# A convolution-attention hybrid block: weighing two score tiles in a row in all eight attentions

## What is computed

```python
# first attention: projections to 32 channels, softmax over 1024 positions, residual
q, k, v = wq @ xf, wk @ xf, wv @ xf                   # (4, 32, 1024)
att = softmax(einsum('bmi,bmj->bij', k, q), axis=2)
x = x + wo @ einsum('bij,bmj->bmi', att, v)
t = x.reshape(4, 64, 1024).transpose(0, 2, 1)         # tokens, 64 channels
# second attention: of the normalised tokens with themselves
u = layernorm(t)
t = t + softmax(einsum('bqd,bkd->bqk', u, u), -1) @ u
# experts: top 2 of 8, gates from a softmax over router logits
w = layernorm(t)
top_p, top_i = top_k(softmax(w @ router_w + router_b), 2)
t = t + sum over the two of (top_p / sum(top_p)) * (w @ expert_w[e] + expert_b[e])
out = t.transpose(0, 2, 1).reshape(4, 64, 32, 32)
```

## Time and profile before

| | us |
|---|---|
| median of 3 runs | 241.38 |
| lowest and highest run | 240.24, 241.77 |
| the profiled execution, as a run | 242.07 |
| its span in the trace | 240.4 |
| TensorE matmuls busy | 215.7 |
| VectorE busy | 152.1 |
| ScalarE busy | 110.1 |
| GpSimd busy | 72.2 |

### The profile page before, as it was taken

One profiled execution on the slowest core, in us unless ns is written; L12 is line 12 of the kernel. 1 busy time (PEld: TensorE's weight loads), 2 busy tenths in 40 slices (PEclk: granted clock), 3 DMA queues, 4 the chain that ended last, 5 costly groups with the idle time before them and its releaser, 6 DMA issues.

```text
span 240.4 us, 2786 instructions
## 1 busy us (share of the span) xinstructions
PE 215.7 (90%) x987; PEld 100.9 (42%) x987; DVE 152.1 (63%) x364; ACT 110.1 (46%) x170; POOL 72.2 (30%) x88
## 2 busy tenths in 40 slices
PE   6999899899999998999899989999899996775494
PEld 1645344635343454243245433433433433353383
DVE  2689766568169686328965994484745365999070
ACT  2533545667854736564435266564546652020101
POOL 8030000160303000300333584003876300774940
PEclk9999999999999999999999999999999999988778
DMA  4770000000000000000000001000000200000021
GB/s 98 134 176 0 3 0 0 0 4 1 0 0 0 3 0 0 0 3 0 1 0 0 3 1 44 0 3 0 0 0 0 48 0 0 0 0 0 0 46 44
DMA packets 3341, 3.67 MB, mean 15 GB/s; under 512 B 2176, under 2 KB 2432, under 8 KB 3328
## 3 DMA queue, kind: packets, MB, share of 16 engines
q1 hardware_dynamic: 3328, 3.50, 6.8%
HBM read 2.45 MB, written 1.05 MB: 15 GB/s over the span
## 4 chain that ended last, share of the span: by engine, by line
PE 66%; DVE 19%; ACT 6%; issue 3%; POOL 3%; DMA 2%; SPq 0%; DVEq 0%; POOLq 0%
PE acc L498 24%; PE ring L491 7%; PE ring L473 6%; PE ring L550 5%; DVE rowmax L1059 5%; PE ring L551 4%; PE ring L592 2%; DVE prod L1200 2%; ACT prob L868 2%; PE ring L593 2%; DMA xin<-in_x 2%; PE ring L537 2%; PE ring L451 2%; PE ring L462 2%; PE ring L463 1%
## 5 line engine op out<-in xcount | busy, mean ns | idle before, releaser
L868 ACT ACTIVATE prob<-ring,shift 128x1024 f32<-128x1024 f32 x32 | 35.6, 1113 | 41.8 <-PE ring L551 41.8
L1059 DVE TENSOR_REDUCE rowmax<-ring 128x1 f32<-128x1024 f32 x32 | 38.2, 1219 | 10.1 <-PE ring L473 10.0
L373 POOL TENSOR_TENSOR sm<-sm,minus_half 128x8 f32<-128x8 f32 x8 | 15.8, 1974 | 86.7 <-DVE sm L1102 86.7
L865 ACT ACTIVATE prob<-ring 128x1024 f32<-128x1024 f32 x32 | 32.4, 1023 | 17.6 <-PE ring L491 17.5
L498 PE MATMUL acc<-prob,val 128*64 128x512 f32 x128 | 34.3, 616 | 2.4 <-ACT prob L865 2.4
L498 PE MATMUL acc<-prob,u 128*64 128x512 f32 x128 | 34.5, 618 | 0.3 <-ACT prob L868 0.3
L1200 DVE TENSOR_TENSOR prod<-ring,gate 128x1024 f32<-128x1024 f32 x16 | 19.3, 1218 | 14.5 <-PE ring L593 14.5
L550 PE MATMUL ring<-zst 128*128 128x512 f16 x64 | 24.6, 385 | 1.2 <-DVE rowmax L1059 1.2
L551 PE MATMUL ring<-zsw,zst 128*128 128x512 f16 x64 | 24.3, 379 | 0.0
L491 PE MATMUL ring<-kst,qst 98*128 98x512 f32 x64 | 21.7, 428 | 1.7 <-DVE kst L1072 1.2
L473 PE MATMUL ring<-qst,kst 96*128 96x512 f32 x64 | 22.6, 439 | 0.1
(11 more groups left out here) (152 smaller groups left out, 319.7 us busy)
## 6 DMA issues: line engine op xcount, KB each, us to landing
xin<-in_x SPq DMA_DIRECT2D x8, 256.0 KB, 4.1
out<-ob SPq DMA_DIRECT2D x6, 128.0 KB, 2.4
e_in<-in_L_ffn_expert_w SPq DMA_DIRECT2D x2, 128.0 KB
out<-ob SPq DMA_DIRECT2D x4, 64.0 KB, 2.0
eb_in<-in_L_ffn_expert_b SPq DMA_DIRECT2D x8, 2.0 KB
wo<-in_L_conv_wo SPq DMA_DIRECT2D x2, 8.0 KB, 2.4
r_in<-in_L_ffn_router_w SPq DMA_DIRECT2D x2, 2.0 KB
w<-in_L_conv_wq SPq DMA_DIRECT2D x1, 16.0 KB, 3.5
```

The source lines that it names most:

```text
L373: pool.tensor_tensor(sm[:, 3, :], sm[:, 2, :], minus_half[:, :], ALU.pow).then_inc(s_rs, 1)
L865: act.activation(prob1[:, j % DEEP, :], flat(filled(act, f"st{j}", b)), ACT.Exp).then_inc(s_p1, 1)
L868: act.activation(prob2[:, j % DEEP, :], flat(filled(act, f"s{j}", b)), ACT.Exp, bias=shift[:, :], accum_out=rsum2[b % 2][:, j:j + 1]).then ...
L1059: dve.tensor_reduce(rowmax[:, tile:tile + 1], flat(filled(dve, f"mx{tile}", b)), AX.X, ALU.max).then_inc(s_mx, 1)
```

## The change

Two weighings are put in a row everywhere, and the next two score tiles are placed ahead of each pair. `weigh_pair1` and `weigh_pair2` call `weigh1` and `weigh2` twice. The new order is written out for all stages; per pair (j, j + 1) it is: score tile j + 1, score tile j + 2, weighings j and j + 1. What was threaded in between stays in the same place of the ring's order, with one exception in FIRST, where a score tile and a maximum tile change places. The function `sixteen`, which nothing called, is removed. The lists of ScalarE, VectorE, GpSimd and SyncE are the same. The core of the diff:

```diff
-FIRST = [("st0", 0), ("st1", 0), ("mx0", 1), ("st2", 0), ("mx1", 1), ("mx2", 1), ("st3", 0), ("mx3", 1), ("st4", 0),
+FIRST = [("st0", 0), ("st1", 0), ("mx0", 1), ("st2", 0), ("mx1", 1), ("st3", 0), ("mx2", 1), ("mx3", 1), ("st4", 0),
...
+            def weigh_pair1(b, j):
+
+                weigh1(b, j)
+                weigh1(b, j + 1)
+
+            def weigh_pair2(b, j):
+                weigh2(b, j)
+                weigh2(b, j + 1)
...
             max_scores(1, 0)
-            weigh1(0, 0)
             scores1(0, 2)
+            weigh_pair1(0, 0)
             max_scores(1, 1)
-            weigh1(0, 1)
-            for j in range(3, T - 1):
-                max_scores(1, j - 1)
-                scores1(0, j)
-                weigh1(0, j - 1)
+            scores1(0, 3)
+            max_scores(1, 2)
+            max_scores(1, 3)
+            scores1(0, 4)
+            weigh_pair1(0, 2)
+            max_scores(1, 4)
+            scores1(0, 5)
+            max_scores(1, 5)
+            scores1(0, 6)
+            weigh_pair1(0, 4)
             max_scores(1, 6)
             scores1(0, 7)
             max_scores(1, 7)
-            weigh1(0, 6)
-            weigh1(0, 7)
+            weigh_pair1(0, 6)
...
             scores1(1, 0)
-            for j in range(1, 3):
-                scores1(1, j)
-                weigh1(1, j - 1)
+            scores1(1, 1)
+            scores1(1, 2)
+            weigh_pair1(1, 0)
             project_qk("q", 2)
             scores1(1, 3)
-            weigh1(1, 2)
             project_qk("k", 2)
             scores1(1, 4)
-            weigh1(1, 3)
+            weigh_pair1(1, 2)
             project_v(2)
             scores1(1, 5)
-            weigh1(1, 4)
             u_transposed(0)
...
+            max_scores(2, 0)
+            scores2(0, 2)
+            weigh_pair2(0, 0)
+            max_scores(2, 1)
+            scores2(0, 3)
+            max_scores(2, 2)
+            scores2(0, 4)
+            weigh_pair2(0, 2)
             max_scores(2, 3)
             scores2(0, 5)
             project_qk("q", 3)
             u_transposed(1)
-            weigh2(0, 4)
             max_scores(2, 4)
             scores2(0, 6)
+            weigh_pair2(0, 4)
             project_qk("k", 3)
-            weigh2(0, 5)
             max_scores(2, 5)
             scores2(0, 7)
             max_scores(2, 6)
-            weigh2(0, 6)
             max_scores(2, 7)
             project_v(3)
-            weigh2(0, 7)
+            weigh_pair2(0, 6)
...
                 scores1(b, 0)
-                for j in range(1, T):
-                    scores1(b, j)
-                    weigh1(b, j - 1)
-                    if b == 3 and j == 3:
-                        y_transposed(0)
-                    if j == 5:
-                        w_transposed(b - 2)
+                scores1(b, 1)
+                scores1(b, 2)
+                weigh_pair1(b, 0)
+                scores1(b, 3)
+                if b == 3:
+                    y_transposed(0)
+                scores1(b, 4)
+                weigh_pair1(b, 2)
+                scores1(b, 5)
+                w_transposed(b - 2)
+                scores1(b, 6)
+                weigh_pair1(b, 4)
+                scores1(b, 7)
                 route(b - 2)
...
             att2_transposed(2)
-            for j in range(2, T):
-                weigh2(3, j - 2)
-                scores2(3, j)
...
-            weigh2(3, 6)
-            weigh2(3, 7)
+            scores2(3, 2)
+            weigh_pair2(3, 0)
+            scores2(3, 3)
+            y_transposed(1)
+            scores2(3, 4)
+            weigh_pair2(3, 2)
+            scores2(3, 5)
+            w_transposed(2)
+            scores2(3, 6)
+            weigh_pair2(3, 4)
+            route(2)
+            scores2(3, 7)
+            weigh_pair2(3, 6)
```

## The result

The changed kernel takes 237.27 us (median of 4 runs, 236.11 to 238.88), the kernel before 240.81 (4 runs, 240.19 to 241.77): ratio 0.985, 95% interval 0.981 to 0.989. A second timing, of six runs beside eleven, gave 237.13 and 241.55: 0.981, interval 0.978 to 0.985; the ratio leaves out one slow run on either side (241.03 and 244.46, at a granted clock of 0.95). It is faster by 3.5 to 4.4 us. 235.6 was forecast, the range 232.5 to 240.5.

A forecast was written before the change was run, and what follows sets the result against it. TensorE, busy for 90% of the span, was taken as what matters. Merges save some 9.5 us there; after waits the stages sum to 5.8 off, so 241.4 - 5.8 = 235.6 us, range 232.5 to 240.5.

The forecast's parts named there:

- The price of a merge: TensorE: each of 30 merges of weighings saves 0.35 us, or 0.25 before an fp16 tile.
- Image 0's second attention loses: Waits on row maxima and q's and k's buffers lose 3.2 us there; image 2's score tile 0 comes 2.46 late.
- The four waits: In image 0's second attention, TensorE idles 1.45, 1.3, 1.2 and 0.65 us before tiles whose buffers are not yet free.
- The stages without maxima: First attentions of images 2 and 3, without row maxima: the sum counts gains of 2.5 and 1.9 us.
- The rival that ScalarE delays the second weighing of each pair: In stages without maxima, exponentials keep twelve pairs' second weighings waiting 0.3 us each: 239.2 us; chance 0.16.
- Image 1's second attention and the last two: Second attentions: image 1's gains 0.6 us through three merges; those of images 2 and 3 gain 3.2 together.
- nothing is added: On TensorE and elsewhere: every matmul, exponential and row maximum stays, and as many bytes move.
- Image 0's first attention: Two full cycles lose 0.19 us each through a 0.54 wait on a maximum; shorter end groups return it: 0.
- The sum of 5.8: Gain in us over all stages, 0.0 + 0.8 - 3.2 + 2.5 + 0.6 + 1.9 + 3.2, off the profiled span of 240.4.
- the chance of 0.04 that I gave the clock: Rival: new pauses slow TensorE's clock, losing half the 6.1 us the tail loses: 238.6 us; chance 0.04.
- The rival of no new waits: Transposes, projections and maxima have enough slack, so all merges reach the end: 231.9 us; chance 0.10.
- the slower one: VectorE stops TensorE a further 3.2 us each in image 0's first, images 1's and 2's second attentions: 245.2; chance 0.08.

The follow-up runs named there:

- the fillers: Changed kernel with dummy matmuls (6, 4, 4 and 2) ahead of the four waiting tiles of image 0's second attention: 237.29 us, ratio 0.982 to the kernel before.

## Why the prediction was right, and where it was off

**The price of a merge** is right. 1.87 for a pair, 0.34 per merge in image 2, where three were undone, and 0.35 was forecast. In image 3 the same three gave only 0.22 each, in part because there they cover a wait.

**Image 0's second attention loses** is right in place, cause and size: +2.64 with the stage before it, +2.4 forecast; score tile 0 of image 2 came at 95.05. The four waits are 3.9 in all, where 4.6 were forecast. The experiments name the same two causes as the forecast: the maxima behind the statistics, and the buffers of q and k.

**The stages without maxima** are right: -2.54 and -2.19 against -2.5 and -1.95. There were no waits before the out projections. The rival that ScalarE delays the second weighing of each pair fell: with the third tile ahead only the first pair of such a stage and the very last one wait (0.28 to 0.30); without it one more does (0.65).

**Image 1's second attention and the last two** fell 0.4 and 0.3 short. Two steps failed. The first is "nothing is added": I took `expert_bias` as one more full-width matmul. It contracts over 64 rows, and going into and out of it costs as with the weighings. Before the change it stood directly ahead of a weighing, after it alone between two full-width tiles. Moving it back ahead of a pair returned 0.14 in image 1's stage and 0.37 in the last two, 0.21 of that by the switch.

The second is the size of a wait in image 1's stage. For its third merge the prediction had a net gain of 0.2, with waits of 0.1 to 0.3 on the exponential, the split and the product. The stretch from maximum tile mx5 to the end of the last weighing takes 6.84 (130.41 to 137.25), before 6.55: a loss of 0.3. The maximum tiles mx6 and mx7, which a weighing had parted, now stand in a row, and mx7 starts 0.99 behind mx6, because its buffer is still being read by VectorE's product of an expert tile:

```profile
133.60 0.73 PE L473 MATMUL ring<-qst,kst 96*128 96x512 f32 x2 [0.17 <-DVE prod L1205]
```

No run takes this wait away, so that it accounts for the rest of the shortfall is read from this trace alone.

**Image 0's first attention** was forecast at 0 and lost 0.2: the wait for the maximum was rightly forecast, but the full cycle takes 4.57, not 4.49.

**From the profile to the time.** Here lies half of the miss of 1.7 us. The sum of 5.8 came out as 4.9 between the first score tile and the last copy; what the median gained is 3.5 in one timing, 4.4 in the other. I made the sum against a span and took the 0.7 between that execution and the median as spread. That was so for the level, but the spread is not symmetric: the changed kernel's fastest runs are at 236.1, and its median 1.0 to 1.2 above. It is the clock in part (the runs' granted clocks go from 0.960 to 0.974), and the chance of 0.04 that I gave the clock was put on one stage, where the fillers showed it isn't the usual cause. The two ends of the sum, head and tail, I had called unchanged; each varies by 1.2 to 1.5 between executions of whatever kernel. That the time still fell near the forecast leans on the width of the range, not on a grip on these ends.

**The chances.** Faster by over 1% held. The rival of no new waits (231.9) fell by the four waits; the slower one fell since image 1's second attention kept a gain and image 0's first lost 0.2 and not 3.2.

## What to carry over

Price a reordering stage by stage: give each tile its slot, and ask when the buffer it takes was last read. A run of matmuls of one shape saves the switches, and pays only where something else still covers the readers of the ring; where a slower engine frees the buffers, leave the fine interleaving, as the version with image 0's second attention in its old order did (another 1.2%; the first attention's gave 0.2 us). A wait that hangs on another engine's chain is a place to put work that needs no buffer of the ring.

## What the runs showed of the hardware

Going from full-width matmuls to the weighings' half-width ones and back costs 0.35 us: 0.09 on the last matmul before, 0.15 inside, 0.11 on the first fp32 one after, and none of the last if that one is fp16 (0.34 for each of the three merges undone in image 2). A matmul over 64 of the 128 rows has the same 0.11 behind it (0.34 instead of 0.23 to the next start) and 0.10 ahead of it (a maximum tile takes 0.75 before it and 0.65 before an expert tile). The Trainium skill (TensorEngine Tiling (Array Packing), Key Properties) says that changing the tiling mode drains the engine. The price in the rows fits that; no run here shows the draining itself.

The stages between head and tail repeat to 0.1 us from execution to execution when the clock stays at 2.4 GHz, whatever the run's total. Four pauses of 0.5 to 1.25 us within 17 us left the clock high in four of the five profiles with that order and no fillers; in the fifth it fell about 3 us behind the last of them, to 0.5 of full from about 92 to 95 us, and the stage took 1.6 longer. In the head the same eight matmuls take 2.2 us or up to 3.4, in executions of the same code.
